# Attention scores as pairs of 64-row products, with the projection tiles moved beside the V products

## The reference, cut to what matters

```
q, k, v = 16 heads of 64 from layernorm(x) @ Wq, Wkv      # 4 batches x 1024 rows
q, k = rope(q), rope(k)                                    # the first 32 of the 64 dimensions are rotated
sim  = q @ k.T * 64**-0.5                                  # 1024 x 1024 per batch and head, 64 of them
attn = softmax(sim)
out  = (attn @ v) @ Wout + bout
```

## Time and profile before

| | us |
|---|---|
| median of 3 runs | 1556.92 (1556.63 to 1557.19) |
| the profiled execution, its own time | 1557.27 |
| its span, first to last instruction | 1555.5 |
| TensorE busy | 1424.9 (92%) |
| VectorE busy | 1222.0 (79%) |
| GpSimd busy | 977.8 (63%) |
| ScalarE busy | 778.3 (50%) |

### The profile page before, as it was taken

The page is one execution under the profiler, slowest core; times in us unless marked ns, Lnnn a source line. Parts: engine busy times, 40 slices in busy tenths (PEclk is TensorE's granted clock), DMA queues, the critical chain, the costliest instruction groups (busy, mean ns, idle before and its releaser), DMA issues.

```text
span 1555.5 us, 25971 instructions
## 1 busy us (share of the span) xinstructions
PE 1424.9 (92%) x7289; PEld 546.8 (35%) x7289; DVE 1222.0 (79%) x1297; ACT 778.3 (50%) x1512; POOL 977.8 (63%) x501
## 2 busy tenths in 40 slices
PE   3689999999999999999999999999999999998886
PEld 1224333333333333333333333333333333333323
DVE  7787888788788878878788888878887887888744
ACT  3244554545454545555455454545545554544464
POOL 4388766658475665838476574848566584757731
PEclk9799999999999999999999999999999999999999
DMA  5312131221303121120313122031312204031002
GB/s 158 73 26 60 25 76 26 50 54 26 83 14 75 34 57 38 44 65 14 75 34 74 22 54 54 14 79 30 75 21 54 54 20 89 14 75 33 3 15 68
DMA packets 70209, 76.00 MB, mean 49 GB/s; under 512 B 27204, under 2 KB 36936, under 8 KB 69928
## 3 DMA queue, kind: packets, MB, share of 16 engines
...
...
## 4 chain that ended last, share of the span: by engine, by line
PE 56%; DVE 13%; issue 13%; POOL 7%; DMA 5%; ACT 3%; SPq 2%; DVEq 0%; ACTq 0%; POOLq 0%
PE O L388 18%; PE S L376 10%; PE S L377 8%; PE M L397 8%; DVE MX L603 5%; PE TILE L312 5%; DVE SUM L613 4%; DMA QK<-STAGE 4%; POOL SA L676 3%; PE TILE L322 2%; POOL STAGE L663 2%; ACT PF L515 2%; SPq L708 1%; PE TILE L306 1%; PE TILE L330 1%
## 5 line engine op out<-in xcount | busy, mean ns | idle before, releaser
L676 POOL TENSOR_TENSOR SA<-PF 128x1024 f32<-128x1024 f32 x256 | 616.5, 2424 | 372.5 <-DVE SUM L610 279.9
L515 ACT ACTIVATE PF<-S 128x512 f32<-128x512 f32 x1024 | 547.8, 599 | 564.9 <-PE S L377 564.1
L603 DVE TENSOR_REDUCE MX<-M 128x1 f32<-128x1024 f32 x504 | 614.5, 1219 | 229.3 <-PE M L397 229.1
L388 PE MATMUL O<-PF,V 128*64 128x512 f32 x2048 | 497.4, 607 | 0.0
L376 PE MATMUL S<-QK 128*128 128x512 f16 x1024 | 393.1, 384 | 0.0
L377 PE MATMUL S<-QK 128*128 128x512 f16 x1024 | 390.1, 381 | 0.0
L397 PE MATMUL M<-QK 64*128 64x512 f16 x1008 | 221.9, 437 | 65.9 <-DVE MX L603 47.7
L613 DVE TENSOR_TENSOR SUM<-SUM,SA 128x1024 f32<-128x1024 f32 x128 | 248.3, 1939 | 3.6 <-POOL SA L676 3.4
L397 PEld LDWEIGHTS M<-QK 64*128 64x128 f16 x1008 | 72.6, 140 | 370.8 <-DVE MX L603 247.9
L388 PEld LDWEIGHTS O<-PF,V 128*64 128x64 f32 x2048 | 124.5, 136 | 206.4 <-issue 149.8
L376 PEld LDWEIGHTS S<-QK 128*128 128x128 f16 x1024 | 99.9, 98 | 165.3 <-issue 64.2
...
## 6 DMA issues: line engine op xcount, KB each, us to landing
QK<-STAGE SPq DMA_DIRECT2D x128, 256.0 KB, 3.9
QK<-STAGE SPq DMA_DIRECT2D x128, 128.0 KB, 3.1
RB<-den SPq DMA_DIRECT2D x128, 128.0 KB, 3.0
...
RT<-DS SPq DMA_DIRECT2D x128, 2.0 KB, 1.7
...
```

Of the source, the lines that this page charges most:

```text
L388: mm = e.matmul(O[DH * z:DH * z + DH, :], V[:, h, kt * DH:(kt + 1) * DH], PF[:, t % SLOTS, z * HALF:(z + 1) * HALF], start=(kt == 0), stop ...
L515: e.activation(PF[:, t % SLOTS, z * HALF:(z + 1) * HALF], S[:, t % 2, z * HALF:(z + 1) * HALF], ACT.Exp, scale=EXP_SCALE).then_inc(exped, 1)
L603: e.tensor_reduce(MX[:, place % 2, q:q + 1], bank, AX, ALU.max).then_inc(max_read, 1)
L676: e.tensor_tensor(SA[:, (t // 2) % 2, :], PF[:, t % SLOTS, :], PF[:, t % SLOTS + 1, :], ALU.add).then_inc(two_summed, 1)
```

## The change

The four products of a score are no longer stacked. Each is a matmul on 64 rows, and for each the two halves z of the queries go to the two row halves of the array, side by side: eight matmuls of 512 columns per step where there were four. For that the halves of the queries lie on different partitions (QH, QL, with KH and KL on both halves), and the row of maxima and its constants are tiles of their own (MQ, MSC). A unit now takes 128 queries of each half z against half of the keys, with two matmuls of the same shape as before, and VectorE reduces to two numbers (MXP), which a small instruction per head (dve_merge) brings together. Per step there is still one unit. The row of maxima is waited for before the fourth product of a head's first step, not before its first, and goes over in two DMAs. The hand-over has DMAs of 192 KB each where it had 128 and 256.

The order in a step changes. TensorE: on an even step the V products, the tile, the unit, the scores; on an odd step the scores, the unit, the tile. ScalarE takes an even step's tile ahead of the exponentials. VectorE takes the maximum first, then the tile of the same step, then the sums and the normalisation. GpSimd takes the sum of exponentials ahead of the rotation. The tables of tiles move by up to ten steps. The core of the diff:

```diff
-QK_AT = (1, 3, 5, 7, 9, 11, 13, 15)
-V_AT = {8: (1, 0), 10: (1, 1), 22: (0, 0), 24: (0, 1)}
-DEN_AT = {6: 1, 20: 0}
+QK_AT = (0, 2, 4, 7, 9, 11, 13, 15)
+V_AT = {17: (1, 0), 18: (1, 1), 24: (0, 0), 26: (0, 1)}
+DEN_AT = {6: 1, 22: 0}
 INVERT_AT = {9: 1, 23: 0}
-NORM_AT = {16: 1, 26: 0}
-OUT_AT = {17: (1, 0), 19: (1, 1), 28: (0, 0), 30: (0, 1)}
+NORM_AT = {15: 1, 27: 0}
+OUT_AT = {19: (1, 0), 21: (1, 1), 29: (0, 0), 31: (0, 1)}
 SUM_AT = {7: 0, 1: 1, 3: 2}
 
 STATS_AT = {6: 2, 14: 3}
 APPLY_AT = (17, 18, 19, 20, 21, 22)
 BIAS_AT = (19, 21, 23, 24, 27, 28)
-TURN_X0_AT = (21, 23, 25, 26, 27, 29)
-TURN_X_AT = (4, 7, 9, 11, 13, 15)
-DOWN_AT = (12, 14, 16, 18, 21, 23)
+TURN_X0_AT = (21, 23, 25, 27, 28, 30)
+TURN_X_AT = (5, 8, 10, 12, 14, 15)
+DOWN_AT = (11, 13, 20, 23, 25, 27)
 
 HAND_ORDER = [("qk", 3), ("max", 1), ("sums", 1), ("inverse", 1), ("spread", 1), ("max", 2), ("qk", 0),
-              ("qk", 1), ("sums", 0), ("max", 3), ("inverse", 0), ("spread", 0), ("qk", 2), ("max", 4)]
+              ("qk", 1), ("max", 3), ("sums", 0), ("inverse", 0), ("spread", 0), ("qk", 2), ("max", 4)]
...
-        QK = sb("QK", [P, GH, 4, N], F16)
-        KHL = QK[:, :, 0, :]
-        KMH = QK[:, :, 1, :]
-        QHH = QK[:, :, 2, :]
-        QML = QK[:, :, 3, :]
+        QK = sb("QK", [P, GH, 3, N], F16)
+        KH = [QK[0:DH, :, 1, :], QK[DH:P, :, 0, :]]
+        KL = [QK[0:DH, :, 2, :], QK[DH:P, :, 1, :]]
+        QH = [QK[0:DH, :, 0, 0:HALF], QK[DH:P, :, 2, 0:HALF]]
+        QL = [QK[0:DH, :, 0, HALF:N], QK[DH:P, :, 2, HALF:N]]
+        MQ = sb("MQ", [P, GH, HALF], F16)
+        MSC = sb("MSC", [P, P], F16)
         V = sb("V", [P, GH, KT * DH], F32)
...
-        MX = sb("MX", [P, 2, KT], F32)
-        MN = sb("MN", [P, 2, KT], F16)
+        MXP = sb("MXP", [P, 2, 2, 2, KT // 2], F32)
+        MX = sb("MX", [P, 2, 2, KT // 2], F32)
+        MN = sb("MN", [P, 2, 2, KT // 2], F16)
...
         def pe_scores(e, it, t):
+
             n, h, kt = it.step(t), t // KT, t % KT
             keys = slice(kt * P, (kt + 1) * P)
+            for z in range(2):
+                wait(e, exped, 2 * n + z - 3)
+                e.matmul(S[:, t % 2, z * HALF:(z + 1) * HALF], KH[z][:, h, keys], QH[z][:, h, :],
+                         start=True, stop=False)
+            for z in range(2):
+                e.matmul(S[:, t % 2, z * HALF:(z + 1) * HALF], KH[z][:, h, keys], QL[z][:, h, :],
+                         start=False, stop=False)
+            for z in range(2):
+                e.matmul(S[:, t % 2, z * HALF:(z + 1) * HALF], KL[z][:, h, keys], QH[z][:, h, :],
+                         start=False, stop=False)
             if kt == 0:
-                e.wait_ge(max_row, 16 * (it.i * GH + h + 1))
+                e.wait_ge(max_row, ROWS * (it.i * GH + h + 1))
             for z in range(2):
-                rows = slice(z * HALF, (z + 1) * HALF)
-                wait(e, exped, 2 * n + z - 3)
-                e.matmul(S[:, t % 2, rows], KHL[:, h, keys], QHH[:, h, rows], start=True, stop=False)
-                e.matmul(S[:, t % 2, rows], KMH[:, h, keys], QML[:, h, rows],
+                side = slice(DH * z, DH * z + DH)
+                e.matmul(S[:, t % 2, z * HALF:(z + 1) * HALF], MSC[side, :], MQ[side, h, :],
                          start=False, stop=True).then_inc(scored, 1)
...
-            for c in range(2):
-                rows, keys = slice(DH * c, DH * c + DH), slice(c * 512, (c + 1) * 512)
-                mm = e.matmul(bank[:, keys], QHH[rows, place, q:N:KT], (KHL, KMH)[c][rows, place, keys],
-                              start=True, stop=True)
+            part, half = q // 2, q % 2
+            for z in range(2):
+                mm = e.matmul(bank[:, z * HALF:(z + 1) * HALF], QH[z][:, place, part:HALF:KT // 2],
+                              KH[z][:, place, half * 512:(half + 1) * 512], start=True, stop=True)
...
                         pe_values(e, it.step(back), it.i * GH + back // KT, back, it.i)
                     elif not it.first:
                         pe_values(e, it.step(back), it.i * GH - 1, back + STEPS, it.i - 1)
+                pe_tiles(e, it, t)
                 if not (it.last and u >= STEPS):
                     pe_next_unit(e, it, u)
-            pe_scores(e, it, t)
-            pe_tiles(e, it, t)
-            if t % 2 == 1 and not (it.last and u >= STEPS):
-                pe_next_unit(e, it, u)
+                pe_scores(e, it, t)
+            else:
+                pe_scores(e, it, t)
+                if not (it.last and u >= STEPS):
+                    pe_next_unit(e, it, u)
+                pe_tiles(e, it, t)
...
+        def act_rots(e, it, t):
             for n, kind, args in it.at(t - 3):
...
-            e.wait_ge(max_read, KT * (head + 1))
-            wait(e, max_row, 16 * (head - 1))
-            e.activation(MN[:, place % 2, :], MX[:, place % 2, :], ACT.Copy, scale=-1.0 / MSCALE).then_inc(max_found, 1)
+            e.wait_ge(max_merged, head + 1)
+            wait(e, max_row, ROWS * (head - 1))
+            e.activation(MN[:, place % 2, :, :], MX[:, place % 2, :, :], ACT.Copy,
+                         scale=-1.0 / MSCALE).then_inc(max_found, 1)
...
-            act_tiles(e, it, t)
+            if t % 2 == 1:
+                act_tiles(e, it, t)
+            act_rots(e, it, t)
...
-            for n, kind, args in it.at(t - 1):
+            for n, kind, args in it.at(t):
...
-            e.tensor_reduce(MX[:, place % 2, q:q + 1], bank, AX, ALU.max).then_inc(max_read, 1)
+            e.tensor_reduce(MXP[:, place % 2, q % 2, :, q // 2], bank.rearrange("p (z n) -> p z n", z=2), AX,
+                            ALU.max).then_inc(max_read, 1)
+
+        def dve_merge(e, head, place):
+
+            e.wait_ge(max_read, KT * (head + 1))
+            e.tensor_tensor(MX[:, place % 2, :, :], MXP[:, place % 2, 0, :, :], MXP[:, place % 2, 1, :, :],
+                            ALU.max).then_inc(max_merged, 1)
...
+            if not (it.last and u >= STEPS):
+                dve_max(e, it.step(u), it.i * GH + u // KT, (u // KT) % GH, u % KT, M[:, :])
+            if u % KT == 0 and not (it.last and u > STEPS):
+                dve_merge(e, it.i * GH + u // KT - 1, (u // KT - 1) % GH)
             dve_tiles(e, it, t)
...
-            if not (it.last and u >= STEPS):
-                dve_max(e, it.step(u), it.i * GH + u // KT, (u // KT) % GH, u % KT, M[:, :])
...
+            if t % 2 == 0 and (not it.first or t > 0):
+                back = t - 2
+                head, part = it.i * GH + back // KT, (back % KT) // 2
+                pool_sum(e, back % STEPS, it.i * (STEPS // 2) + back // 2, 3 * head + (-1, 0, 1, 1)[part])
             for n, kind, args in it.at(t - 4):
                 if kind == "proj" and args[2] == "rot":
                     rot_low(e, args, it.i + 1)
             for n, kind, args in it.at(t - 1):
                 if kind == "proj" and args[2] == "rot":
                     rot_add(e, args, it.i + 1)
-            if t % 2 == 0 and (not it.first or t > 0):
-                back = t - 2
-                head, part = it.i * GH + back // KT, (back % KT) // 2
-                pool_sum(e, back % STEPS, it.i * (STEPS // 2) + back // 2, 3 * head + (-1, 0, 1, 1)[part])
...
-                sp.dma_start(QK[top, h, 0:3:2, :], STAGE[rows, 1:3, t, :]).then_inc(handed[h], 16)
-                sp.dma_start(QK[low, h, 0:4, :], STAGE[rows, 0:4, t, :]).then_inc(handed[h], 16)
+                sp.dma_start(QK[top, h, :, :], STAGE[rows, 0:3, t, :]).then_inc(handed[h], 16)
+                sp.dma_start(QK[low, h, :, :], STAGE[rows, 1:4, t, :]).then_inc(handed[h], 16)
...
-            row = QML[0:1, place, :].rearrange("o (p t) -> o p t", t=KT)
-            sp.dma_start(row, MN[:, place % 2, :]).then_inc(max_row, 16)
+            for z in range(2):
+                row = MQ[DH * z:DH * z + 1, place, :].rearrange("o (p t) -> o p t", t=KT // 2)
+                sp.dma_start(row, MN[:, place % 2, z, :]).then_inc(max_row, 16)
```

More of the change, by code:

```diff
@@ L28 @@
 HAND = 4 * 16
+ROWS = 2 * 16
 PV_LAG = 4
@@ L169, in build @@
         DOWN = STAGE[:, 0:2, :, :].rearrange("p a b c -> p (a b c)")
-        H = [QK[:, h, :, :].rearrange("p a b -> p (a b)").bitcast(F32) for h in range(2)]
-        QT = QK[:, 3, :, :].rearrange("p a b -> p (a b)").bitcast(F32)
+        LATE = QK[:, :, :, :].rearrange("p h a b -> p (h a b)").bitcast(F32)
+        H = [LATE[:, h * 4 * 512:(h + 1) * 4 * 512] for h in range(2)]
+        QT = LATE[:, 8 * 512:12 * 512]
         S = pb("S", [P, 2, N], F32)
@@ L193, in build @@
         handed = [sem(f"handed{h}") for h in range(GH)]
-        unit_made, max_read, max_found, max_row = (sem(n) for n in ("unit_made", "max_read", "max_found", "max_row"))
+        unit_made, max_read, max_merged, max_found, max_row = (
+            sem(n) for n in ("unit_made", "max_read", "max_merged", "max_found", "max_row"))
         scored, exped, pv_done, o_copied = sem("scored"), sem("exped"), sem("pv_done"), sem("o_copied")
```

(30 more changed lines are left out.)

3 lines of the change are left out of this document (removed).

## The result

The changed kernel takes 1627.99 us (median of 4 runs, 1626.79 to 1629.3) where the kernel before takes 1557.06: a ratio of 1.0453 (95% interval 1.0435 to 1.0471). It is slower by 71 us; 1611 was forecast, with a range of 1565 to 1662.

The account below looks back on a forecast made before the run. TensorE bounds the kernel, with waits for VectorE and the hand-over. Stream 68.3 plus waits 4.3 plus long stretch 20.6 make 93.2 us per iteration, 3.6 more; 15 x 3.6 = 54 on 1557.3 gives 1611 us, range 1565 to 1662.

Parts of the forecast that it names:

- The stream: TensorE's own work without waits: 82.0 us per iteration, 2.6 us less than before, bounds 81 to 84.
- Pairs at 0.215 us: Score matmuls on two row halves run side by side, 0.215 us per pair, so a step's products cost the same.
- The changes of form: TensorE switching between matmul shapes: 0.10 or 0.155 us each; 4.0 us per iteration go at the units, 1.8 return.
- The long stretch: From step 15's odd unit to step 20's unit: 20.6 us against 15.3, bounds 18.5 to 21.
- The last term: TensorE at step 20 waits 1.4 us more for the hand-over, at the end of the stretch from step 15.
- rival B: The forecast plus a clock fall after step 18's wait: 1.6 to 3.0 us per iteration, 1635 to 1656 us; chance 0.18.
- The over-runs elsewhere: VectorE late at steps 3, 4, 7, 9, 11, 13, 25, 27: 6.2 us listed, 4.3 taken per iteration, bounds 1.5 to 7.
- the odd unit's slack: Between even and odd units only two steps' scores, 1.94 us, remain, so VectorE may be 0.2 us late.
- A: Waits stay as they are because engines have idle time: 1515 us, up to 1550 with some more waits; chance 0.12.
- D: Gain and loss cancel within 0.2% of the kernel before; chance 0.03.
- C: Score pairs don't run side by side in long chains: 0.4 us per step, some 200 us, 1800 us; chance 0.04.
- The last iteration and what follows it: The end of the launch, without projections of q and k: given no change in the forecast.

Follow-up runs that it names:

- k: The changed kernel with VectorE's sums and normalisation ahead of the maximum, and tile 13's rotation ahead of GpSimd's sum of exponentials at step 14: 1522 us.
- f: The changed kernel with the merge of the maxima as a reduction of one operand instead of an operation on two: 1628 us.

## Why the prediction was right

**The stream.** Pairs at 0.215 us: right. The changes of form came out as 0.10 both into and out of 64 rows, where I had 0.155 for the way out, so tiles beside the V products cost what I took. The stream is 82.5 us in k against 82.0 forecast. That it came so near is in part luck. My 5.0 us of waits per iteration had single waits of the start in them (6.5 and 5.8 us); in the loop it is 4.0, so the old stream was 85.5 and not 84.6, and the form and the new places save 3.0 us and not 2.6. The gain of 42 us that I gave to unchanged waits is 35 in k, whose waits per iteration are nearly those of before (4.2 and 4.0).

**The long stretch.** 20.6 forecast, 20.8 measured. SUM0 4.0 and 3.8, P2 7.5 and 7.2, rotation 11.0 and 10.6, V copy 13.3 and 12.7, low part 14.5 and 14.0. The V tile waited 3.25 where I had 4.0. The last term, 1.4 us of waiting for the hand-over at step 20, is there only in the two iterations without half clock, with 0.9 us and a stretch of 20.1 to 20.2. In the others half the clock stretched TensorE's own work between 871.4 and 874.6 and filled that time, as rival B had it.

**The over-runs elsewhere.** 4.3 us taken. By the steps' lengths against the shortest like step, step 5 had 1.1 (half of it the merge's, by f), step 9 0.2, step 11 0.9, step 13 0.7, step 25 0.3, step 27 0.9 and step 29 1.0: 5.1 in all, of which 3.9 are waits, and none at steps 3 and 7. The sum was near, the list was not: I let VectorE be held by P0 and P3 at places where GpSimd had been done earlier, and did not have step 29. Without half clock an iteration takes 93.4 us against 93.2 forecast.

**Which part.** I called the stretch GpSimd's and made the odd unit's slack a second item. The runs weigh them otherwise. Putting VectorE's sums and normalisation ahead of the maximum again gives 80 us, undoing the one rotation 25, both together 106: they add up, and VectorE's part is three quarters. The prediction's chain has both in it (SUM0 last in step 15, then P2 ahead of the rotation), but its words name GpSimd first.

**The rivals.** A fails, since the new waits of the long stretch came where they were worked out, and D with it. B holds in kind and not in size: the clock fell in eleven iterations of thirteen, but an iteration takes 93.9 us on average and 93.4 where it did not fall, so the fall costs 0.5 us and not 1.6 to 3.0, most of it hidden in the wait for the hand-over. C is out, with pairs 0.215 us apart.

**The 17 us by which the forecast was low.** Over the iterations the loss was 65 us where I had 54, and the clock is about 7 of those 11. The last iteration and what follows it, to which I gave no change, took 152.7 us where it was 147.0. That term was put at nothing without a row for it; no run here takes it apart (k has 148.8).
